# A hybrid transformer block on one core: the second expert matrices kept on chip, experts unpacked ahead of waits, other jobs, and constant matmuls in planned gaps

## What is computed

```python
x = x + attn_a(layernorm(x))     # 11 dyadic scales x 4 taps of shifted keys and values, gated
x = x + ffn(layernorm(x))        # 8 experts, each position goes to its best one
x = x + attn_b(layernorm(x))     # h = tanh(h @ A.T + x_t @ B.T), 512 steps one after the other
x = x + ffn(layernorm(x))        # the same experts again

def ffn(x):                      # top1 = argmax(x @ Wg.T)
    h = gelu(x @ W1[e] + b1[e])  # 128 -> 512
    y = h @ W2[e] + b2[e]        # 512 -> 128, only for positions with top1 == e
```

## Time and profile before

| what | us |
|---|---|
| median of 3 runs (lowest, highest) | 1520.73 (1519.0, 1521.88) |
| the profiled execution, whole | 1523.29 |
| its span, first to last instruction | 1521.5 |
| PE busy in the span | 1118.4 (74%) |
| DVE busy | 809.2 (53%) |
| POOL busy | 776.5 (51%) |
| ACT busy | 654.8 (43%) |

### The profile page before, as it was taken

The page is one execution under the profiler, slowest core; times in us unless marked ns, Lnnn a source line. Parts: engine busy times, 40 slices in busy tenths (PEclk is TensorE's granted clock), DMA queues, the critical chain, the costliest instruction groups (busy, mean ns, idle before and its releaser), DMA issues.

```text
span 1521.5 us, 31460 instructions
## 1 busy us (share of the span) xinstructions
PE 1118.4 (74%) x9456; PEld 809.5 (53%) x9456; DVE 809.2 (53%) x1741; ACT 654.8 (43%) x2052; POOL 776.5 (51%) x1258
## 2 busy tenths in 40 slices
PE   3666688687679868789897689846796968665743
PEld 1233355444356655566664457645675756555642
DVE  4788788878878887667787553301122212212000
ACT  2233455353346645545663336424453524333421
POOL 2554445774865566863648885444314154433111
PEclk9677799778589989989996669967997966679967
DMA  4800233000224434322322034545564644446653
GB/s 125 264 1 0 85 100 85 20 2 3 71 75 113 114 113 114 112 81 71 106 78 74 25 95 119 152 127 164 145 164 119 168 108 131 124 132 168 187 142 90
DMA packets 146228, 158.37 MB, mean 104 GB/s; under 512 B 18532, under 2 KB 92557, under 8 KB 146061
## 3 DMA queue, kind: packets, MB, share of 16 engines
q1 hardware_dynamic: 135296, 138.89, 33.1%
q0 software_dynamic: 8192, 16.79, 3.7%
q10 hardware_dynamic: 2573, 0.69, 0.2%
HBM read 124.97 MB, written 31.33 MB: 103 GB/s over the span
## 4 chain that ended last, share of the span: by engine, by line
PE 39%; POOL 19%; issue 11%; DVE 10%; ACT 7%; another core or an unknown queue 6%; SPq 4%; DMA 2%; ACTq 1%; DVEq 1%; POOLq 0%
POOL acc L699 11%; PE bank L1020 9%; PE bank L1028 7%; PE bank L1055 4%; PE bank L959 3%; POOL back L726 2%; POOL mom L664 2%; PE bank L915 2%; PE bank L927 2%; DVE term L1212 2%; POOL sorted_x L715 2%; PE bank L1000 1%; ACT hT L870 1%; PE bank L986 1%
## 5 line engine op out<-in xcount | busy, mean ns | idle before, releaser
L699 POOL TENSOR_TENSOR acc<-acc,term 128x512 f32<-128x512 f32 x219 | 289.2, 1321 | 67.2 <-DVE term L1212 46.2
L870 ACT ACTIVATE hT<-bank,b1T 128x128 f32<-128x128 f32 x736 | 220.4, 372 | 170.0 <-PE bank L1020 130.3
L1020 PE MATMUL bank<-xTb,w1b 128*128 128x128 f32 x1472 | 260.1, 317 | 32.5 <-ACT xTb L858 19.5
L1028 PE MATMUL bank<-w2b,hT 128*128 128x128 f32 x1472 | 256.8, 313 | 21.8 <-ACT hT L870 14.7
L1319 DVE TENSOR_TENSOR ysb<-bank,b2bc 128x128 f32<-128x128 f32 x184 | 53.0, 288 | 400.9 <-PE bank L1028 295.0
L1020 PEld LDWEIGHTS bank<-xTb,w1b 128*128 128x128 f32 x1472 | 220.6, 219 | 53.4 <-ACT xTb L858 28.7
L1028 PEld LDWEIGHTS bank<-w2b,hT 128*128 128x128 f32 x1472 | 218.7, 217 | 45.3 <-ACT hT L870 23.6
L726 POOL DMA_INDIRECT back<-sorted_y,slot_i x128 | 127.4, 996 | 175.1 <-DMA sorted_y<-ysb 83.2
L1055 PE MATMUL bank<-hid,abcT 128*32 128x16 f32 x4096 | 139.1, 202 | 95.1 <-ACT hid L890 72.5
L890 ACT ACTIVATE hid<-bank 128x16 f32<-128x16 f32 x512 | 94.3, 184 | 264.9 <-PE bank L1055 196.7
L1055 PEld LDWEIGHTS bank<-hid,abcT 128*32 128x32 f32 x4096 | 89.1, 118 | 208.8 <-ACT hid L890 117.8
(11 more groups left out here) (160 smaller groups left out, 1623.0 us busy)
## 6 DMA issues: line engine op xcount, KB each, us to landing
w1b<-in_W SPq DMA_DIRECT2D x184, 256.0 KB
w2b<-w_rows SPq DMA_DIRECT2D x184, 256.0 KB
xsb<-sorted_x SPq DMA_DIRECT2D x184, 64.0 KB
sorted_y<-ysb SPq DMA_DIRECT2D x184, 64.0 KB
X<-in_x SPq DMA_DIRECT2D x64, 64.0 KB
sorted_x<-K SPq DMA_DIRECT2D x16, 256.0 KB, 3.8
out_x<-X SPq DMA_DIRECT2D x64, 64.0 KB
w_rows<-normal SPq DMA_DIRECT2D x1, 2048.0 KB, 8.7
```

Of the source, the lines that this page charges most:

```text
L699: nc.gpsimd.tensor_tensor(acc[:], acc[:] if k > 1 else term[0][:], term[k % NTERM][:], ALU.add).then_inc(S["terms_added"], 1)
L870: last = nc.scalar.activation(tile(hT[u], c), tile(bank[4 + u], c), ACT.Gelu, bias=b1T[:, ds(e * HC + c, 1)])
L1020: last = nc.tensor.matmul(tile(bank[4 + n % 2], c), tile(w1b[n % W_RING], c), xTb[n % 2][:], start=True, stop=True, skip_group_check=True)
L1028: last = nc.tensor.matmul(bank[4 + n % 2][:, 0:D], tile(hT[n % 2], c), tile(w2b[n % W_RING], c), start=(c == 0), stop=(c == HC - 1), skip_ ...
```

## The change

**Jobs.** The eight jobs take other chunks. Their tiles were 8, 20, 20, 20, 28, 12, 12, 8; now they are 16, 12, 16, 16, 16, 12, 24, 16. The slots are 184 as before. The first job holds chunks 0 to 3 (it held 0 and 1). The last two jobs hold second-pass chunks only, 6 to 11 and 12 to 15; they were 11 to 13, and 14 and 15.

**Second matrices.** W2 is read once into `w2`, 16 KB in each partition, and stays. The copy to `w2_rows`, its load for each slot (`loadv`), the ring `w2b` and the waits on them go. `result` reads the slot's matrix out of `w2` at an address in a register, so PE now loads the packed words too, once a job, and computes one register for each slot and one for each matmul.

**Unpacking.** On PE, ACT and DVE the register with the slot's expert is computed before the waits of `result`, `gelu` and `yadd` (`held`), where ACT and DVE computed it behind them.

**Space.** `normal` shrinks from eight chunks to four (`xnj`). The chunks of the last two jobs (preparations 22 to 31, `LATE`) are normalised into the space of V, and their first matrices land in a ring of eight buffers in the space of K (`LATE_RING`). Both wait for the last reads of K and V, `LAST_READS`.

**Constant matmuls.** `fillings()` finds gaps of more than 0.5 us in PE's planned queue and puts matmuls of 256 columns on the constant `esel` there, into a bank whose last reader is done; 65% of the gap is filled. There are 505 in 100 places: 389 in 57 places ahead of the first recurrence step, 46 in 17 places between the first and the last step, 70 in 26 places behind it.

**Order.** `PE_PACE` goes from 0.86 to 0.93, and with the new jobs the plan gives every queue a new order. Three places of it follow; columns are the line and what is written from what is read.

```diff
@@ -40,8 +40,8 @@
...
-JOB = [job(range(0, 2), range(0, 0)), job(range(2, 7), range(0, 0)), job(range(7, 10), range(0, 2)), job(range(10, 14), range(2, 3)),
-       job(range(14, 16), range(3, 8)), job(range(16, 16), range(8, 11)), job(range(16, 16), range(11, 14)), job(range(16, 16), range(14, 16))]
+JOB = [job(range(0, 4)), job(range(4, 7)), job(range(7, 10), range(0, 1)), job(range(10, 13), range(1, 2)),
+       job(range(13, 15), range(2, 4)), job(range(15, 16), range(4, 6)), job((), range(6, 12)), job((), range(12, 16))]
@@ -54,8 +54,13 @@
...
-W_RING, X_RING, XN_RING = 3, 4, 8
-PE_PACE = 0.86
+W_RING, LATE_RING, X_RING, XN_RING = 3, 8, 4, 4
+PE_PACE = 0.93
+IDLE_US, FILL_US, FILL_SHARE, FREE_US = 0.5, 0.15, 0.65, 1.0
+LATE_JOB = 6
+LATE = CHUNKS_BEFORE[LATE_JOB]
@@ -247,10 +256,11 @@
...
-        old = JOB_OF_PREP[p - XN_RING] if p >= XN_RING else None
+        old = JOB_OF_PREP[p - XN_RING] if XN_RING <= p < LATE else None
...
-                  [("pmom", p, 0)] + ([("scatter", old, JOB[old].tiles - 1)] if old is not None else []))
+                  [("pmom", p, 0)] + ([("scatter", old, JOB[old].tiles - 1)] if old is not None else [])
+                  + (LAST_READS if p >= LATE else []))
@@ -284,9 +294,11 @@
...
-        piece("SP", "loadw", s, 0, 0.3, rank, [("texp", n, 0), past("hidden", s - W_RING, 1), past("loadw", s - 1)], lands=3.2)
-        piece("SP", "loadv", s, 0, 0.3, rank, [("texp", n, 0), past("result", s - W_RING, 1), past("loadv", s - 1), ("loadw", s, 0)],
-              lands=3.2)
+        late = s - SLOTS_BEFORE[LATE_JOB]
+        ring = LATE_RING if late >= 0 else W_RING
+        piece("SP", "loadw", s, 0, 0.3, rank,
+              [("texp", n, 0), past("loadw", s - 1)]
+              + ([LAST_READS[0]] if 0 <= late < LATE_RING else [past("hidden", s - ring, 1)]), lands=3.2)
@@ -294,7 +306,7 @@
...
-            piece("PE", "result", s, h, 0.68, rank, [("gelu", s, 1), ("loadv", s, 0), ("result", s, 0) if h else None])
+            piece("PE", "result", s, h, 0.68, rank, [("gelu", s, 1), ("result", s, 0) if h else None])
@@ -378,6 +390,42 @@
...
+def fillings():
+    out, end = {}, 0.0
+    reader = {b: None for b in (1, 2, 3, 4, 5, 6, 7)}
+    for key in ORDER["PE"]:
+        what, n, k = key
+        best = None
+        for b, last in reader.items():
+            since = max(end, BEGIN[last] + WORK[last][1] + FREE_US) if last else end
+            if best is None or since < best[0]:
+                best = since, b, last
+        if best and end and BEGIN[key] - best[0] > IDLE_US:
+            out[key] = int((BEGIN[key] - best[0]) * FILL_SHARE / FILL_US), best[1], best[2]
+        if what == "turn":
+            reader.pop(4 + n % 2)
+        elif what == "result" and k == 1:
+            reader[4 + n % 2] = "yadd", n, 0
+        elif what == "rT":
+            reader.pop(6 + n % 2)
+        elif what == "ry":
+            reader[6 + n % 2] = "rres", n, 0
+        elif what == "qproj":
+            reader[1] = "product", n, len(products(n)) - 1
+        elif what == "reduce" and k == 0:
+            reader.pop(2)
+            reader.pop(3)
+        elif what == "spread" and k >= last_term(n) - 1:
+            reader[2 + k % 2] = "term", n, k
+        end = BEGIN[key] + WORK[key][1]
+    return out
+FILL = fillings()
@@ -579,6 +624,20 @@
...
+        def first_matrix(n):
+            late = n - SLOTS_BEFORE[LATE_JOB]
+            if late < 0:
+                return w1b[n % W_RING][:], w1_in[n % W_RING], 16 * (n // W_RING + 1)
+            u = late % LATE_RING
+            return K[:, u * NH:(u + 1) * NH], w1_late_in[u], 16 * (late // LATE_RING + 1)
+        def normalised(p):
+            return xnj[p % XN_RING] if p < LATE else V[:, (p - LATE) * CW:(p - LATE + 1) * CW]
+        def held(eng, value, top):
+            return eng.snap(eng.to_reg(value), min_val=0, max_val=top)
@@ -606,28 +665,22 @@
...
-            sp.dma_start(normal[:, 0:NE * HC * D].rearrange("p (e c d) -> p e c d", e=NE, c=HC),
+            sp.dma_start(w2[:].rearrange("p (e c d) -> p e c d", e=NE, c=HC),
...
-            sp.wait_ge(S["w2_in"], 16)
-            sp.dma_start(w2_rows.rearrange("(e p) x -> p e x", p=P),
-                         normal[:, 0:NE * HC * D].rearrange("p (e x) -> p e x", e=NE)).then_inc(S["w2_laid"], 16)
...
+                    late = n - SLOTS_BEFORE[LATE_JOB]
+                    ring = LATE_RING if late >= 0 else W_RING
...
-                    if n >= W_RING:
-                        sp.wait_ge(S["hidden_ready"], nth("hidden", n - W_RING, 1))
+                    if late == 0:
+                        sp.wait_ge(S["products_ready"], nth("product", CHUNKS - 1, len(products(CHUNKS - 1)) - 1))
+                    elif n >= W_RING and not 0 < late < LATE_RING:
+                        sp.wait_ge(S["hidden_ready"], nth("hidden", n - ring, 1))
...
-                    sp.dma_start(w1b[n % W_RING][:], a["W1"][ds(e, 1), :, :].rearrange("a d h -> (a d) h")).then_inc(
-                        w1_in[n % W_RING], 16)
-                elif what == "loadv":
-                    if n == 0:
-                        sp.wait_ge(S["w2_laid"], 16)
-                    if n >= W_RING:
-                        sp.wait_ge(S["y_psum"], nth("result", n - W_RING, 1))
-                    e = sp.value_load(te_i[:, n:n + 1], min_val=0, max_val=NE - 1)
-                    sp.dma_start(w2b[n % W_RING][:], w2_rows[ds(e * P, P), :]).then_inc(w2_tile_in[n % W_RING], 16)
+                    buf, landed, _ = first_matrix(n)
+                    sp.dma_start(buf, a["W1"][ds(e, 1), :, :].rearrange("a d h -> (a d) h")).then_inc(landed, 16)
@@ -840,13 +892,13 @@
...
-                        if n == 0:
-                            act.wait_ge(S["w2_laid"], 16)
-                        if n >= XN_RING:
+                        if n >= LATE:
+                            act.wait_ge(S["terms_ready"], nth("term", CHUNKS - 1, last_term(CHUNKS - 1)))
+                        elif n >= XN_RING:
...
-                    normalise(xnj[n % XN_RING], chunk_x(CHUNK_OF_PREP[n]), prs[u][:, k:k + 1], pnm[u][:, k:k + 1],
+                    normalise(normalised(n), chunk_x(CHUNK_OF_PREP[n]), prs[u][:, k:k + 1], pnm[u][:, k:k + 1],
@@ -861,14 +913,14 @@
...
-                    e = expert(words[j], j, n)
...
+                        bias[n] = held(act, expert(words[j], j, n) * HC, (NE - 1) * HC)
...
-                                                    bias=b1T[:, ds(e * HC + c, 1)])
+                                                    bias=b1T[:, ds(bias[n] + c, 1)])
@@ -915,7 +967,16 @@
...
+            words, second = {}, {}
...
+                if (what, n, k) in FILL:
+                    times, b, reader = FILL[what, n, k]
+                    if reader:
+                        signal = {"yadd": "y_ready", "rres": "r_sum", "product": "products_ready", "term": "terms_ready"}
+                        pe.wait_ge(S[signal[reader[0]]], nth(*reader))
+                    for _ in range(times):
+                        nc.tensor.matmul(bank[b][:, 0:256], tile(esel, 0), esel[:, 0:256], start=True, stop=True,
+                                         skip_group_check=True)
@@ -1013,20 +1074,26 @@
...
+                    w1, landed, so_far = first_matrix(n)
...
-                        pe.wait_ge(w1_in[n % W_RING], 16 * (n // W_RING + 1))
+                        pe.wait_ge(landed, so_far)
...
-                        last = nc.tensor.matmul(tile(bank[4 + n % 2], c), tile(w1b[n % W_RING], c), xTb[n % 2][:],
-                                                start=True, stop=True, skip_group_check=True)
+                        last = nc.tensor.matmul(tile(bank[4 + n % 2], c), tile(w1, c), xTb[n % 2][:], start=True, stop=True,
+                                                skip_group_check=True)
...
+                    j = JOB_OF_SLOT[n]
+                    if j not in words:
+                        pe.wait_ge(S["w2_in"], 16)
+                        pe.wait_ge(S["tiles_ready"], j + 1)
+                        words[j] = packed_experts(pe, j)
...
+                        second[n] = held(pe, expert(words[j], j, n) * (HC * D), (NE - 1) * HC * D)
...
-                        pe.wait_ge(w2_tile_in[n % W_RING], 16 * (n // W_RING + 1))
...
-                                                tile(w2b[n % W_RING], c), start=(c == 0), stop=(c == HC - 1),
+                                                w2[:, ds(second[n] + c * D, D)], start=(c == 0), stop=(c == HC - 1),
@@ -1312,11 +1379,11 @@
...
-                    e = expert(words[j], j, n)
+                    e = held(dve, expert(words[j], j, n) * D, (NE - 1) * D)
...
-                    V_.tensor_tensor(ysb[u][:], bank[4 + u][:, 0:D], b2bc[:, ds(e * D, D)], ALU.add).then_inc(S["y_ready"], 1)
+                    V_.tensor_tensor(ysb[u][:], bank[4 + u][:, 0:D], b2bc[:, ds(e, D)], ALU.add).then_inc(S["y_ready"], 1)
```

18 lines of the change are left out of this document (8 added, 10 removed).

## The result

The changed kernel takes **1502.97 us** (median of 4 runs, 1500.02 to 1508.19) against 1521.31 for the kernel before (1519.0 to 1533.54): the ratio is 0.985, 95% interval 0.981 to 0.988, 18 us less. Forecast were 51 us less, 1470. The direction was right and the time lies in the range of 1410 to 1514, but the change is a third of what I expected of it. Measured twice more it gave 0.984 and 0.982.

What follows compares the result with a forecast made beforehand. The bound was taken as a chain: recurrence start, steps, two gather stops, slots left, last gather. Terms summed along it to 1470.5, plus 1.8 gives 1472.3 against 1523.3, 51 less; from the median 1470 us, range 1410 to 1514.

Steps and rivals of the forecast that it cites:

- Seven recurrence chunks in one row at 41.5: 290: Recurrence chunks 0 to 6 run unbroken at 41.5 us each, 290 us, from 465 to 755.
- about one chunk of the first layer without steps: between 50 and 54 us, I take 50: Before recurrence chunk 7: the recurrence pauses for about one first-layer chunk, 50 us, until 805.
- Chunks 7 to 9: Recurrence: these three take 116 us, as the three ending at 968 before, and end at 921, 47 us earlier.
- Chunks 0 to 8: First layer: chunk 5 ends at 296, chunks 6 to 8 take 54 us each to 458, recurrence starts at 465.
- The stop before chunk 10: Recurrence waits 45 us instead of 106, with 8 slots left in it; largest term, 61 us less.
- Chunks 10 to 15: Recurrence: with 50 slots and about 70 indirect transfers, again 291 us, ending at 1257.
- The last 41 results: Behind the recurrence: 173 us, plus 21 for transfer rows, less 12 of store waits, 182, ending at 1439.
- The registers: Unpacking ahead of waits: between 0.2 us won and lost a slot, 8 us either way at the end; taken as nothing.
- K and V as buffers: Late jobs' waits on chunk 15's last product and term: nothing, or at most a few us.
- The order is too tight: Rival: late gathers stop PE's queue at chunks 4, 7 and 10; 1510 us, range 1490 to 1516, chance 0.17.
- The rows get cheap: Rival: fewer bytes shorten stops beside POOL's gather rows, chunks 10 to 15 and end; 1390 us, 1380 to 1430, chance 0.17.
- The lower clock, and slower: Rival: PE stays at the lower level in chunks 10 to 15 and the last slots; together 1588 us, chance 0.09.

Runs made afterwards that it cites:

- the table alone: Kernel before with only the new table of jobs: 1510.11 us, 0.990 of the kernel before on a chip with stops; 1.002 on one without.
- the spaced kernels: Changed kernel with short POOL additions behind 92 indirect transfers and PE_PACE 0.86, one also with POOL's additions first: 1.002 and 1.006 of the kernel before, without stops.

## Why the prediction was wrong, point by point

**What bounds the kernel.** The chain I named is the right one (start of the recurrence, its steps, its stops for a gather, the slots left, the last gather), and so was the last part of it. The step that failed is this sentence: "there the chain of steps sets the pace, and the first layer's last chunks ride along". From it came three terms: "Seven recurrence chunks in one row at 41.5: 290", "about one chunk of the first layer without steps: between 50 and 54 us, I take 50", and "Chunks 7 to 9 as the three that end at 968, 116 us". They measured 311, 70 and 143, together 68 us more than forecast; all other terms together came 37 us better. That the time lies inside the range is partly luck: the two errors have opposite signs.

The rows to see it were there. Recurrence chunks do take 41.5 us beside the first layer, but the first layer pays for them: its chunks 12 to 15 took (923 - 621) / 4 = 75.5 us each with steps beside them, against 215 / 4 = 54 without. I moved the recurrence forward until it lay beside the first layer from its chunk 9 on, and charged nothing for it. By these two rates the chunks 9 to 15, six with steps beside them and one in the stop, cost 6 x 75.5 + 54 = 507 us. In the changed kernel they take 511, from 440 to 951, though single ones take between 57 and 86. From the end of chunk 8, my own 458, the last residual add would have been forecast for 965. PE's queue has the last output of the first layer in the first half of recurrence chunk 9, so chunk 9 could not have ended at my 921; it would have come after 965, and the 47 us that I had it ahead of before were gone on paper. It measured 975.

The second half of the same error: the stop before chunk 7 isn't one chunk of the first layer, it is the end of job 2. Beside steps a slot takes 332 / 36 = 9.2 us in the trace of before (36 results between 636 and 968 us). In all 18 traces with the new table job 2's last add ends between 793 and 810 us, and its first gather starts 3.5 to 4.6 us behind that. Chunk 7 then starts between 821 and 847 us, though chunk 0 of the recurrence starts between 428 and 464 in them. A recurrence that starts earlier only waits longer here: at pace 0.86, where chunks 0 to 6 end earliest, the stop is 99 us.

The excess of the first term lies in one place. Chunks 0 to 6 but for chunk 3 take 39 to 42 us each; chunk 3 takes 60, with 4 slots beside it. It takes 38 at pace 0.86 with no slot beside it, but 50 and 52 in the table alone, which has none beside it either, so slots alone don't explain it.

**Chunks 0 to 8.** 296 and 465 were forecast, 293 and 451 came. The early clock rose from 0.80 to 0.91, and the constant matmuls won 3 us here, as taken. Chunks 6 to 8 took 147 us, 49 a chunk, where I had carried over 54.

**Chunks 7 to 9**, forecast 116, are 143 us in the first trace and 132 and 134 in two other executions of the same kernel. Chunk 8 took 47 us at clock 0.61 in the first and 37 and 38 at 0.91 and 0.82 in the others, so about 10 of the 27 us belong to that execution, with its lower clock. For the other 17 the first layer is not a shown cause: with the table alone the three chunks take 118 and 122 us, and at pace 0.86 without constant matmuls 124 to 129. At pace 0.93 without constant matmuls it is 136 and 138, so a part goes with the order; what in it makes the chunks slow is open.

**The stop before chunk 10**: 47 us for 45. Moving slots out of it works as told: 8 results are left in it.

**Chunks 10 to 15**: 286 for 291, with 50 results as forecast. That the transfers' price stayed was right on this chip. On chips without stops the same chunks take 239 us (changed kernel without constant matmuls), so it held only where the chip has the stops.

**The last 41 results**: 165 for 182. The mis-sized term is the second matrices' loads. I took 12 of 20 us of waits on stores back. Without that the sum gives 173 + 21 = 194, and the table alone measured 193 for 42 results; there those waits are 51.6 us, since more slots stand there. 43 of them go, and the stage is 28 us shorter: 28 where I had 12. The changed kernel differs from the table alone in its other parts too; in the one series that has both without these, the waits fall from 63.7 to 24.2 us and the stage from 166 to 147. The trace of before couldn't show the 51.6. That the waits left are 8.1 us, as many as I left, is luck.

**The registers** cost nothing that shows, and won between nothing and 9 us in all, inside the bound. **The planner's pace** I had counted as part of the order and given no price, without a reason; the runs with 0.86 put it at 5 to 16 us. **K and V as buffers**: no wait on the last product or term shows in the changed kernel's chain.

**The rivals.** "The order is too tight", 1490 to 1516, holds the measured time, and its places were half right: the time is lost between chunk 3 and chunk 9. Its mechanism is not what happened, though: longer stops at chunks 4 and 10 didn't come (gaps of 0.4 and 47 us), only the one at chunk 7 did, and chunks 3 and 7 to 9 were slow rather than stopped. "The rows get cheap" fell: stops stayed at 137 to 166 us with 32% fewer bytes. The Trainium skill (DMA: Bandwidth & Descriptors, Issuing engines are not separate DMA queues) says that transfers run on the same 16 DMA engines and interleave, whichever engine issued them. No run here shows otherwise, but the stops that this rival was about fell to 57 and 35 us when other work stood between POOL's transfers, not with fewer bytes. "The lower clock, and slower" fell: the last stages had 0.79 and 0.86.

**What stays open.** What sets the 73 us of a first-layer chunk (511 / 7) beside the recurrence. It is not the transfers between additions (taken out, given back), and whether it is PE's work the clock kept hidden. And why ACT and DVE stop beside POOL's unbroken rows on some chips and not on others: shown is only that they do, and that a short instruction in between, with the slower pitch that it brings, ends most of it.

## What to carry to other kernels

When a chain of small steps is moved beside another stage, read the price from the other stage: 41 us a chunk was true of most steps, but the layer that "rides along" paid 20 us a chunk. When a table of places and a saving in bytes come together, cost each with the other in place: the table alone was worth 0 to 17 us here, and the loads that it had made critical were worth more with it than the old trace showed. A row of indirect transfers from one queue is worth breaking up with a short instruction, if the trace shows engines idle beside it without a releaser; try it, since on chips without such stops the spaced kernels gained nothing.

## What was not expected of the hardware

- Chips differ by 7% on one kernel: 1418 to 1419 us in two series and 1520 to 1529 in four. Three kernels that were traced on both sorts have nearly the same first 1000 us (12 to 32 us apart) and a mean clock that is 0.02 to 0.04 lower on the slower sort (the table alone: 0.85 and 0.83). What stands out behind that is idle time of ACT and DVE beside unbroken rows of POOL's indirect transfers at a pitch of 1.25 us: 137 to 206 us of it in ten traces on one sort of chip, 0 to 3 in eight on the other.
- One addition of 128x128 on POOL behind each of 92 such transfers took the stops from 137 to 166 us down to 57, and 35 to 40 us off the kernel; the same of 128x512 took them to 35 us, but the longer rows cost more than that.
- With 497 of 4559 matmuls in 520 us left out, the granted clock was 0.75 instead of 0.86, and the time stayed the same.
- With 368 constant matmuls in the first 291 us the clock there was 0.89 instead of 0.77, worth 3 us there.
